# Per-token norm in the first stage: load, norm and gates of a linear attention as one block

## The reference, cut to what matters

```python
x = L0_attn_x                                  # 16 x 256 x 128
x = x + L0_attn(_layernorm(x))                 # linear attention, 32 heads of 4, two states a head
x = x + L0_ffn(_layernorm(x))                  # 8 experts, top 2
x = x + L1_attn(_layernorm(x))                 # retention
x = x + L1_ffn(_layernorm(x))                  # windowed attention and MLP, depth 2

# within L0_attn, x being the normed input:
beta = clip(sigmoid(x @ Wbeta.T + bbeta), 0.85, 0.9995)   # 64 columns of decay
mix = softmax((x @ Wmix.T + bmix).reshape(b, t, 32, 2))   # two shares, a sigmoid of the difference
# scan over time with beta as decay, then divided, mixed, projected, normed
```

## Time and profile before

| | us |
|---|---|
| median of three runs | 1468.37 |
| runs | 1466.29, 1468.37, 1468.88 |
| span of the profiled execution | 1407.0 |
| median less span | 61.4 |

### The profile page before, as it was taken

How to read it: one execution, slowest core, us unless ns; L and a number is a source line. 1 busy time by engine, 2 the same in 40 slices (tenths; PEclk the granted TensorE clock), 3 DMA queues, 4 the chain that set the end, 5 groups by cost and what they waited for, 6 DMA issues and landing times. The chain is left out here.

```text
span 1407.0 us, 26525 instructions
## 1 busy us (share of the span) xinstructions
PE 1211.5 (86%) x7852; PEld 790.4 (56%) x7852; DVE 1044.5 (74%) x2575; ACT 884.2 (63%) x2302; POOL 841.7 (60%) x774
## 2 busy tenths in 40 slices
PE   6879999973777999399689999998978999999797
PEld 3333344422556888234367777774656777777465
DVE  1289999885797998456488888874648888888564
ACT  6623333332444665067489989996648898899674
POOL 0045443514771666331788888886658887788663
PEclk9899999985898999589799999999999999999999
DMA  4800000001321221410000000000000000000001
GB/s 111 288 1 0 1 0 1 1 0 58 106 93 65 71 73 56 161 35 0 23 1 3 2 0 1 0 2 1 1 23 2 2 3 1 1 0 1 1 1 60
DMA packets 35021, 43.99 MB, mean 31 GB/s; under 512 B 5620, under 2 KB 24977, under 8 KB 34912
## 3 DMA queue, kind: packets, MB, share of 16 engines
q1 hardware_dynamic: 30304, 34.27, 7.5%
q0 software_dynamic: 4608, 8.47, 1.9%
HBM read 22.65 MB, written 21.12 MB: 31 GB/s over the span
## 5 line engine op out<-in xcount | busy, mean ns | idle before, releaser
L2099 DVE TENSOR_TENSOR R<-bank,tab 128x1024 f32<-128x1024 f32 x128 | 156.0, 1224 | 70.2 <-ACT sq L2009 69.4
L2043 ACT ACTIVATE W<-W,nm 128x128 f32<-128x128 f32 x512 | 198.3, 393 | 0.4
L1797 POOL TENSOR_TENSOR R<-R 128x512 f32<-128x512 f32 x128 | 161.1, 1280 | 16.0 <-DVE R L2099 16.0
L2122 DVE CUSTOM_DVE_ANT_0 W<-bank,mask_q,rn 128x128 f32<-128x128 f32 x512 | 147.5, 345 | 17.4 <-PE bank L1918 12.8
L1812 POOL TENSOR_TENSOR W<-W,rden 128x512 f32<-128x512 f32 x128 | 132.5, 1040 | 40.6 <-DVE rden L2129 35.2
L1308 POOL DMA_INDIRECT expert_rows<-Yt,xin x80 | 82.6, 1032 | 67.8 <-DVE Yt L1281 49.8
L1011 POOL DMA_INDIRECT expert_slots<-tok_rows,dst x64 | 67.5, 1054 | 66.4 <-ACT tok_rows L1035 45.6
L2043 ACT ACTIVATION_READ_ACCUMULATOR W<-W,nm 128x1 f32 x512 | 98.7, 193 | 0.0
L2027 ACT ACTIVATE QK<-bank 128x512 f32<-128x512 f32 x128 | 75.1, 587 | 35.6 <-PE bank L1893 33.7
L726 DVE TENSOR_TENSOR_SCAN S<-beta,U 128x512 f32<-128x512 f32 x64 | 93.5, 1483 | 0.0
L1943 PE MATMUL bank<-PT,VA 128*64 128x128 f32 (+1 forms) x1024 | 85.8, 261 | 3.7 <-ACT PT L2051 2.8
(11 more groups left out here) (350 smaller groups left out, 3481.2 us busy)
## 6 DMA issues: line engine op xcount, KB each, us to landing
expert_slots<-empty SPq DMA_DIRECT2D x8, 650.0 KB, 6.6
xin<-expert_slots SPq DMA_DIRECT2D x8, 650.0 KB, 4.0
expert_rows<-empty SPq DMA_DIRECT2D x8, 512.0 KB, 6.7
pair_rows<-expert_rows SPq DMA_DIRECT2D x16, 256.0 KB, 4.4
expert_raw<-w1e_dram SPq DMA_DIRECT2D x9, 256.0 KB, 2.9
expert_raw<-w2e_dram SPq DMA_DIRECT2D x9, 256.0 KB, 3.2
tok<-x_dram SPq DMA_DIRECT2D x8, 256.0 KB, 4.7
out_dram<-tok_out SPq DMA_DIRECT2D x8, 256.0 KB, 2.6
```

Source lines behind the costliest of these rows:

```text
L1797: nc.gpsimd.tensor_tensor(halves[:, :, 0, :, z, :], halves[:, :, 0, :, z, :], halves[:, :, 1, :, 1 - z, :], ALU.add).then_inc(summed, 1)
L2043: m = nc.scalar.activation(x, x, ACT.Exp, scale=-1.0, bias=nm[:, p % RING, j:j + 1], accum_out=den[:, p % RING, j:j + 1])
L2099: nc.vector.tensor_tensor(R[:, i, qk, :, :].rearrange("p c (h d) -> p c h d", d=DH), x, y.to_broadcast([P, 2, HEADS, DH]), ALU.mult).then_ ...
L2122: m = nc.vector.tensor_tensor_reduce(W[:, p % RING, j * P:(j + 1) * P], ps[BS[i]][:, cols], k.const["mask_q"][:, cols], rn[:, par, 2 * s + ...
```

## The change

The three blocks become one. Tokens are normed as they stand after loading, one token to a partition: DVE takes `bn_stats` (six numbers for a tile's row of 128) and `bn_aggr` (mean and variance), ACT takes Ln and Exp of a 128x4 column block, DVE scales the tile into `tok_normed`. PE turns each tile twice, raw (bank 0, copied by ACT to `k.XT`) and normed (bank 1, copied by DVE to `k.H`). Each load has a semaphore of its own. The gates' three products follow per chunk in the same block, with banks 2 to 4 and 5 to 7 in turn. The 16 clearing DMAs are issued in the scan's block. Loops over chunks are written out.

```diff
-            for n in range(NT):
-                if n % 16 == 0:
-                    pe.wait_ge(x_in[n // 16], 16 * (4 + (n == 0)))
-                if n % 4 == 0 and n >= 8:
-                    pe.wait_ge(stored, n // 4 - 1)
-                t = nc.tensor.transpose(k.ps[(n // 4) % 2][:, (n % 4) * P:(n % 4 + 1) * P], tok[:, n, :], k.const["ident"][:])
...
-            load(k)
-            norm_stage(k, "n0", 0, norm_sems, w0)
             linear_attention(k, w0)
...
+                for q in range(NCH):
+                    sp.dma_start(tok[:, 4 * q:4 * q + 4, :], xf[:, 4 * q:4 * q + 4, :]).then_inc(x_in[q], 16)
+                for n in GATE_WEIGHTS:
+                    sp.dma_start(w[n][:], k.dram[n]).then_inc(gate_in, 16)
+                for n in SCAN_WEIGHTS:
+                    sp.dma_start(w[n][:], k.dram[n]).then_inc(k.weights_in, 16)
...
+                def turn_input(q):
+                    pe.wait_ge(x_in[q], 16)
+                    if q > 0:
+                        pe.wait_ge(x_kept, q)
+                    for t in range(4):
+                        m = nc.tensor.transpose(ps[BX][:, t * P:(t + 1) * P], tok[:, 4 * q + t, :], k.const["ident"][:])
+                    m.then_inc(x_turned, 1)
+
+                def turn_normed(q):
+                    pe.wait_ge(normed, q + 1)
+                    if q > 0:
+                        pe.wait_ge(h_kept, q)
+                    for t in range(4):
+                        m = nc.tensor.transpose(ps[BH][:, t * P:(t + 1) * P], tokn[:, 4 * q + t, :], k.const["ident"][:])
+                    m.then_inc(h_turned, 1)
+
+                def gate(c):
+                    bank = gate_bank(c)
+                    pe.wait_ge(h_kept, c + 1)
+                    if c > 1:
+                        pe.wait_ge(gates, 4 * (c - 1))
+                    for m in range(M0):
+                        nc.tensor.matmul(ps[bank + m][:], w["wbeta"][:, m, :], k.H[:, chunk(c)], start=True, stop=True)
+                    nc.tensor.matmul(ps[bank + 2][:], wmixd[:], k.H[:, chunk(c)], start=True, stop=True).then_inc(logits, 1)
+
+                pe.wait_ge(ident_in, 16)
+                for q in range(AHEAD):
+                    turn_input(q)
+                turn_normed(0)
+                for q in range(AHEAD, NCH):
+                    turn_input(q)
+                pe.wait_ge(gate_in, 16 * len(GATE_WEIGHTS))
+                pe.wait_ge(diff, 3)
+                for c in range(NCH):
+                    if c + 1 < NCH:
+                        turn_normed(c + 1)
+                    gate(c)
...
+                for q in range(NCH):
+                    keep_input(q)
+                    root(q)
                 nc.scalar.preload_act_table(ACT.Sigmoid)
...
+                def moments(q):
+                    dve.wait_ge(x_in[q], 16)
+                    for n in range(4 * q, 4 * q + 4):
+                        i = nc.vector.bn_stats(stats[:, n, :], tok[:, n, :])
+                    i.then_inc(stats_r, 1)
+                    dve.wait_ge(stats_r, q + 1)
+                    for n in range(4 * q, 4 * q + 4):
+                        i = nc.vector.bn_aggr(mv[:, n, :], stats[:, n, :])
+                    i.then_inc(mean_r, 1)
+
+                def scale(q):
+                    dve.wait_ge(rstd_r, q + 1)
+                    for n in range(4 * q, 4 * q + 4):
+                        i = nc.vector.tensor_scalar(tokn[:, n, :], tok[:, n, :], mv[:, n, 0:1], rs[:, n:n + 1], ALU.subtract, ALU.mult)
+                    i.then_inc(normed, 1)
+
+                def keep_normed(q):
+                    dve.wait_ge(h_turned, q + 1)
+                    nc.vector.tensor_copy(k.H[:, chunk(q)], ps[BH][:]).then_inc(h_kept, 1)
...
             @block.sync
             def _(sp):
+                for e in range(NE):
+                    sp.dma_start(k.xs[e * CAP:(e + 1) * CAP, :].rearrange("(p t) w -> p t w", p=P), empty[:]).then_inc(k.cleared, 16)
...
                 sp.wait_ge(k.cleared, 16 * N_CLEAR)
...
+            nc.gpsimd.sem_clear(range(k.first_spent, k.scan_spent + 1))
...
-            nc.gpsimd.sem_clear(range(k.first_spent, k.last_spent + 1))
+            nc.gpsimd.sem_clear(range(k.scan_spent + 1, k.last_spent + 1))
```

More of the change, by code:

```diff
@@ L85, in wait_alone @@
     eng.wait_ge(sem, value)
[L89 to L126, removed]
 ROUTING = ["wr", "iota8", "slotbase", "tokid", "tri", "ones"]
@@ L373, in _ @@
-                for q in range(2 * T // (8 * P)):
-                    sp.dma_start(k.ys[q * 8 * P:(q + 1) * 8 * P, :].rearrange("(p t) w -> p t w", p=P),
-                                 empty[:, 0:8, 0:P]).then_inc(k.cleared, 16)
             @block.tensor
             def _(pe):
-                pe.wait_ge(k.weights_in, 16 * len(WEIGHTS0))
-                pe.wait_ge(diff, 3)
-                with pe.Fori(0, NCH // 2) as c2:
-                    for i in range(2):
-                        c, bank = 2 * c2 + i, 4 * i
-                        pe.wait_ge(gates, c * 4 + 4)
-                        for m in range(M0):
-                            nc.tensor.matmul(ps[bank + m][:], w["wbeta"][:, m, :], k.H[:, chunk(c)], start=True, stop=True)
-                        nc.tensor.matmul(ps[bank + 2][:], wmixd[:], k.H[:, chunk(c)], start=True, stop=True).then_inc(logits, 1)
@@ L391, in _ @@
+                pe.wait_ge(const_in, 16 * (N_FIRST - 1))
+                pe.wait_ge(x_kept, NCH)
+                nc.tensor.matmul(ps[BX][:, 0:P], w["wout0"][:], k.const["centre"][:], start=True, stop=True).then_inc(wout_mm, 1)
+                nc.tensor.matmul(ps[BH][:, 0:1], k.const["centre"][:], w["vec0"][:, 4:5], start=True, stop=True).then_inc(wout_mm, 1)
             @block.scalar
             def _(act):
-                act.sem_inc(gates, 8)
+                nc.scalar.preload_act_table_set(LNEXP)
@@ new lines, in scale, with clip @@
+                def scale(q):
[6 more added lines that the diff above has]
+                    nc.vector.tensor_copy(k.H[:, chunk(q)], ps[BH][:]).then_inc(h_kept, 1)
+                def clip(c):
+                    dve.wait_ge(gates, 4 * c + 2)
+                    for m in range(M0):
+                        nc.vector.tensor_scalar(beta[m][:, chunk(c)], beta[m][:, chunk(c)], BMIN, BMAX,
+                                                ALU.max, ALU.min).then_inc(clipped, 1)
@@ L412, in _ @@
+                for q in range(AHEAD):
+                    moments(q)
+                scale(0)
+                for q in range(AHEAD, NCH):
+                    moments(q)
+                keep_normed(0)
+                dve.wait_ge(gate_in, 16 * len(GATE_WEIGHTS))
                 nc.vector.tensor_tensor(wmixd[:], w["wmix"][:, 0, :], w["wmix"][:, 1, :], ALU.subtract).then_inc(diff, 1)
@@ L414, in _ @@
                 nc.vector.tensor_tensor(bd[:, 1:2], w["vec0"][:, 3:4], w["vec0"][:, 2:3], ALU.subtract).then_inc(diff, 1)
-                with dve.Fori(0, NCH) as c:
-                    dve.wait_ge(gates, c * 4 + 10)
-                    for m in range(M0):
-                        nc.vector.tensor_scalar(beta[m][:, chunk(c)], beta[m][:, chunk(c)], BMIN, BMAX,
-                                                ALU.max, ALU.min).then_inc(clipped, 1)
+                for q in range(1, NCH):
+                    scale(q)
+                    keep_normed(q)
+                    if q > 2:
+                        clip(q - 3)
+                for c in range(NCH - 3, NCH):
+                    clip(c)
                 dve.wait_ge(wout_mm, 2)
-                nc.vector.tensor_copy(wout[:], ps[3][:, 0:P])
-                nc.vector.tensor_copy(bout[:], ps[7][:, 0:1])
+                nc.vector.tensor_copy(wout[:], ps[BX][:, 0:P])
+                nc.vector.tensor_copy(bout[:], ps[BH][:, 0:1])
                 dve.wait_ge(clipped, 2 * NCH)
```

143 lines of the change are left out of this document (55 added, 88 removed).

## The result

On the chip of the timed comparison the changed kernel takes 1450.49 us (median of 4 runs, 1449.61 to 1451.51), the kernel before 1467.33 (4 runs, three of them at 1466.29 to 1468.88 and one at 1459.57, which nothing here explains). The ratio is 0.9898, with a 95% interval of 0.9873 to 0.9923: 16.8 us less, where 14.9 were predicted. The first four experiments ran where the kernel before took 1467.68 us; the others came from two chips where everything is some 58 us shorter (the first experiment shows where). There the changed kernel took 1390.15 us and the one before 1409.23, 19.1 less, ratio 0.9872 (0.9850 to 0.9894). So I compare ratios across chips, and microseconds only within one chip, or up to the routing block: the way from the scan's first matmul to it takes 94.7 us in the changed kernel's profiles from either kind of chip.

The account below looks back on a forecast made before the run. The scan's start at 64.1 us was the question, with the gates PE-bound. One stage would start it at 49.2, 14.9 less, so 1468.4 - 14.9 = 1453.5 us, range 1447.5 to 1461.5.

Parts of the forecast that it names:

- rival 1: Gates: PE bounds them, giving 1453.5 us, own range 1450.5 to 1456.5; chance 0.60.
- Turning 1.81 a chunk: Input turning: with one bank, each chunk is a full PE, ACT, PE loop of 1.81 us.
- DVE's moments 1.36 a chunk: DVE before the first gate: bn_stats at 0.21, bn_aggr at 0.10 and 0.12 for waits make 1.36 us a chunk.
- case 2: DVE before the first gate: small instructions cost their whole duration, first gate 5.1 us later, time 1458.6; chance 0.20.
- Scaling 0.92: DVE before the first gate: scaling four tiles takes 0.92 us, priced at one element a cycle.
- First gate 19.3: Start of the gates: PE turns until 19.1 us, so the first gate comes at about 19.3.
- PE ends at 46.3: Gates: PE needs 27.0 us, including 2.1 and 0.5 for half clock and turning near the first chunk, ending at 46.3.
- Scan at 49.2: Border to the scan: last activations end at 48.9 us, border 0.33, so the scan starts at 49.2, not 64.1.
- Rival 3, the clock stays full: PE before and in the gates and scan's opening: full clock saves 20.0 us in all, time 1448.4; chance 0.13.
- Clears hidden: Scan: clearing DMAs issued there delay nobody, with cover of over 60 us before the first copy of logits.
- It is eaten elsewhere: Scan's opening or its code fetch: the clears' transfers stretch it, time 1466 to 1471; chance 0.03.
- 61.4 us outside the span: Whole kernel: 61.4 us of the 1468.4 us median lie outside the 1407.0 us profiled span, unchanged.

Follow-up runs that it names:

- the first experiment: The kernel before, unchanged, profiled once more (the repeat of the kernel before): 1465.54 us, span 1463.7.
- run 4: The changed kernel with every bn_stats issued a second time into a spare tile, 32 more DVE instructions: 1450.18 us.
- run 8: The changed kernel with raw tiles turned into two banks in turn: alone 1393.36 us; with 32 idle DVE memsets added 1389.75 us, ratio 0.9855.
- run 9: The changed kernel with two banks for raw tiles, the first chunk's gates put first and DVE's work reordered for it: 1394.05 us, ratio 0.9879.
- run 2: The kernel before with only the 16 clearing DMAs moved into the scan's block: 1462.78 us.
- run 6: The changed kernel again, unchanged, on one of the faster chips: 1390.15 us, ratio 0.9872.
- run 10: The changed kernel with PE and DVE waiting for four chunks' loads at a time, as the kernel before did: 1394.80 us.
- run 3: The changed kernel with the 16 clearing DMAs issued in the first block again: 1450.83 us.
- run 5: The changed kernel with 32 small memsets that nothing reads added on DVE at its start: 1390.99 us, ratio 0.9875.
- run 7: The kernel before with 87 small memsets that nothing reads added on DVE in the load (the shifted kernel): 1405.68 us, ratio 0.9971.

## Why the prediction was right

The verdict and the likeliest case (rival 1 of the text, PE bounds the gates) were right, the size 1.9 us short (14.9 for 16.8). Step by step, with the term of the sum, and what it measured:

- *First transpose 4.0*: 4.31.
- *Turning 1.81 a chunk*: 1.87. This loop, not DVE, set the first gate.
- *DVE's moments 1.36 a chunk*: 1.17 to 1.26. bn_stats, that no row of before showed, came at 0.20 apart for the 0.21 taken from its nearest row. DVE was some 1.5 us ahead of PE (runs 4 and 8), where the sum had it level within 0.2, so case 2, small instructions at their whole duration, did not come near. *Scaling 0.92*: 1.0 from start to start. Four tiles take 1.11 us (the DVE row of run 8), one takes 0.34, more than the 0.28 of a bn_stats of the same 128 columns. The Trainium skill, VectorE: DVE Perf Modes (Mode 2×_2P), has two elements a cycle for this kind of instruction. At 128 columns nothing of it is left in the time. At 512 it shows: the clips with constants take 0.42 us, where a tensor_tensor takes 0.69, and from 128 to 512 columns the form with two per-partition operands grows by 0.20 to 0.30 us (0.34 to 0.545 at least, 0.644 in the median), a tensor_tensor by 0.41. So what the one-element price missed here is a fixed part that is dearer than the columns, and the page's rule would not have given the 0.5 us that the prediction works out from it.
- *First gate 19.3*: 19.17. *PE ends at 46.3*: 44.67. The gates took 25.5 us for the 27.0 of the sum. The term that was mis-sized most is the half clock's: I added 2.1 and 0.5 for the first chunk and its turning, the two took 4.79 instead of 3.13, so 1.7. The other 0.6 are small: a chunk took 3.02 to 3.13, not 3.2.
- *Scan at 49.2*: 47.60. The tail behind PE is 2.93 us (2.9 predicted).
- *Rival 3, the clock stays full*: partly true, and I had treated it as one case. In the scan's opening it held in most runs of the changed kernel and not in run 9, for some 2 us by routing, and in run 2 in part. At the first gates it holds in some profiles and not in others (runs 6, 10 and the banks alone of run 8 against the first profile, runs 3, 4, 5, 9 and run 8 with memsets), for 2.5 us between two profiles of the same program. What decides is open in both places.
- *Clears hidden*: right, and 2.1 us of border were theirs (run 2). In the new stage they would have been hidden in either place (run 3).
- *It is eaten elsewhere* (0.03): a part was. Of 18.5 us that the changed kernel is ahead of the repeat of the kernel before where the first layer begins (720.9, 739.4), 14.8 are left at its end (1002.5, 1017.3). This step was missing in the sum. What the runs show is that idle instructions ahead of the layers change their length (runs 5 and 7). That the change's own 3.7 us come from where its program lies is the likely reading, and is not shown: run 5, which took them back in the profile, did not lower the time.
- *61.4 us outside the span*: wrong. 1.8 are outside; the profile was from an execution without the late signals. The sum survived, because the change comes before them.
- *Bounds kept*: the time of the comparison, 1450.5, lies in the range of 1447.5 to 1461.5.

So the size came out near partly by luck, by two errors of opposite sign: 3.8 us too little gain up to routing (14.9 for 18.7), and 3.7 us of loss in the first layer that I had not seen. The profiles of the changed kernel and of the repeat of the kernel before end 14 us apart (spans 1449.7 and 1463.7), the medians 16.8; the 2.8 us between them may be the scatter of single executions; nothing shows it.

## What to carry to other kernels

A stage border costs more than its barrier when one queue's issue ends late (2.1 us here) or when the next stage opens at half clock (some 2 us): look at what every engine, SP too, does in the last microseconds ahead of it. Operations that the trace doesn't show can be priced by the nearest shape in it (bn_stats at 0.20 us for the 0.21 taken). When comparing two profiles, note at which clock a stretch ran before giving its difference to an edit, and cut the whole span into stages, since a change of the program's length can move some microseconds in a loop far behind it: here 0.3% from memsets that nobody reads.

## What the hardware showed

- 87 idle memsets on DVE in the kernel before made it 0.3% faster (0.9971, 0.9961 to 0.9982); the shifted kernel, the one before and the changed one had a first layer of 274.3, 278.0 and 281.6 us, with waits of DVE of 0.67, 2.65 and 3.8 us at one place, after which PE's clock did not fall, fell once, or fell twice.
- The kernel before takes 1467 us on one chip and 1409 on two others. The 58 us lie where POOL issues its indirect DMAs and the other engines wait up to 54.4 us. The cause is open; it was not tried.
- The same program had its clock up before the first gate in one profile and after it in another, 2.5 us apart at the routing block.
- After the same 2.43 us of idle PE opened the scan at full clock in the changed kernel and at half in run 9 (two matmuls in 1.10 and 2.04 us), 1.8 us apart at the routing block.
